# Attention with a LoRA gate, one core: the order of weight splits, low parts and the gate's activation changed

## The reference

```python
xn = _layernorm(x, axis=-1)
# s = attention(xn):
q = rmsnorm(xn @ Wq.T, q_norm_w); k = rmsnorm(xn @ Wk.T, k_norm_w); v = xn @ Wv.T
scores = einsum('bkgqd,bksd->bkgqs', qg, k) / sqrt(HD)
bias = where(rel > 0, NEG_INF, slopes * rel)      # ALiBi, causal
s = (softmax(scores + bias) @ v) @ Wo.T
# g = silu of a mixture of 8 low rank products of xn, weighted by a softmax of a router
g = _silu(_L0_ffn_ref(xn, A, B, Wr, br))
x = x + s * g
```

## Time and profile before

| | before |
|---|---|
| median of 3 runs | 810.39 us (809.46 to 814.38) |
| the profiled execution: its time, its span | 813.82 us, 812.0 us |
| PE busy | 740.5 us (91%) |
| DVE, ACT, POOL busy | 599.1 us (74%), 561.0 us (69%), 403.5 us (50%) |
| DMA, mean share of 16 engines | 63% |
| mean granted clock of TensorE | 0.973 |

### The profile page before, as it was taken

How to read it: one execution, slowest core, us unless ns; L and a number is a source line. 1 busy time by engine, 2 the same in 40 slices (tenths; PEclk the granted TensorE clock), 3 DMA queues, 4 the chain that set the end, 5 groups by cost and what they waited for, 6 DMA issues and landing times.

```text
span 812.0 us, 14699 instructions
## 1 busy us (share of the span) xinstructions
PE 740.5 (91%) x3729; PEld 620.5 (76%) x3729; DVE 599.1 (74%) x1378; ACT 561.0 (69%) x1370; POOL 403.5 (50%) x423
## 2 busy tenths in 40 slices
PE   8888989989899889989899899999899898999787
PEld 7777868867788778878788678877787787887676
DVE  7855677776878778686887769687786768778455
ACT  4665767677677778667676776776685676768763
POOL 5313454456445663554544564544645544446447
PEclk9999999999999999999999899999999999999989
DMA  7014848577485757768486766858476684856732
GB/s 278 1 34 126 272 114 232 165 211 217 128 276 145 230 157 217 205 170 258 116 253 169 197 203 164 263 130 266 133 220 185 179 254 111 264 157 178 237 98 91
DMA packets 214707, 148.27 MB, mean 183 GB/s; under 512 B 48896, under 2 KB 205440, under 8 KB 214528
## 3 DMA queue, kind: packets, MB, share of 16 engines
q1 hardware_dynamic: 214656, 147.77, 63.2%
HBM read 85.84 MB, written 61.87 MB: 182 GB/s over the span
## 4 chain that ended last, share of the span: by engine, by line
PE 31%; issue 20%; DVE 11%; POOL 10%; DMA 10%; ACT 10%; SPq 7%; DVEq 1%; ACTq 0%; POOLq 0%
POOL pt_lo L515 5%; SPq L419 5%; PE qkv_ps L1137 5%; DMA x_sb<-turning 4%; PE qkv_ps L1138 4%; PE qkv_ps L1139 4%; POOL inv_rms L505 3%; ACT probs L633 3%; DMA qk_moved<-turning_qk 3%; PE score_ps L1137 3%; PE score_ps L1139 2%; PE out_ps L1137 2%; PE score_ps L1138 2%; PE out_ps L1138 2%; PE out_ps L1139 2%
## 5 line engine op out<-in xcount | busy, mean ns | idle before, releaser
L515 POOL TENSOR_TENSOR pt_lo<-x_sb,pt_hi 128x512 fp32r<-128x512 f32 x153 | 199.8, 1332 | 229.4 <-ACT pt_hi L677 229.4
L1137 PE MATMUL qkv_ps<-w_hi,xt_hi 128*128 128x512 f32 (+1 forms) x512 | 178.8, 349 | 26.6 <-DVE w_lo L960 19.4
L625 ACT ACTIVATE probs<-probs,neg_max 128x128 f32<-128x128 f32 (+3 forms) x256 | 141.9, 556 | 58.9 <-DVE neg_max L884 56.9
L884 DVE CUSTOM_DVE_ANT_0 probs<-score_ps,cst,slope 128x128 f32<-128x128 f32 (+3 forms) x256 | 131.3, 547 | 63.0 <-PE score_ps L1139 54.2
L1138 PE MATMUL qkv_ps<-w_lo,xt_hi 128*128 128x512 f32 (+1 forms) x512 | 177.2, 346 | 0.0
L1139 PE MATMUL qkv_ps<-w_hi,xt_lo 128*128 128x512 f32 (+1 forms) x512 | 175.9, 343 | 0.0
L1137 PEld LDWEIGHTS qkv_ps<-w_hi,xt_hi 128*128 128x128 f32 x512 | 99.6, 195 | 48.9 <-DVE w_lo L960 22.3
L633 ACT ACTIVATE probs<-probs,recip 128x128 f32<-128x128 f32 (+3 forms) x252 | 122.3, 548 | 9.9 <-DVE recip L891 9.9
L903 DVE STREAM_TRANSPOSE squared<-probs 128x256 f32<-128x256 f32 (+3 forms) x124 | 102.6, 828 | 27.2 <-ACT probs L633 26.7
L1138 PEld LDWEIGHTS qkv_ps<-w_lo,xt_hi 128*128 128x128 f32 x512 | 99.5, 194 | 12.1
L1139 PEld LDWEIGHTS qkv_ps<-w_hi,xt_lo 128*128 128x128 f32 x512 | 99.2, 194 | 11.8
(11 more groups left out here) (157 smaller groups left out, 1424.5 us busy)
## 6 DMA issues: line engine op xcount, KB each, us to landing
turning_qk<-squares SPq DMA_DIRECT2D x240, 80.0 KB, 1.9
qk_moved<-turning_qk SPq DMA_DIRECT2D x60, 320.0 KB, 3.3
turning<-squared SPq DMA_DIRECT2D x120, 128.0 KB, 2.3
x_sb<-turning SPq DMA_DIRECT2D x30, 512.0 KB, 5.1
w_raw<-wqkv SPq DMA_DIRECT2D x32, 384.0 KB, 5.5
turning<-squared SPq DMA_DIRECT2D x120, 96.0 KB, 1.9
x_sb<-turning SPq DMA_DIRECT2D x30, 384.0 KB, 4.3
turning<-squared SPq DMA_DIRECT2D x128, 64.0 KB, 1.7
```

Of the source, the lines that this page charges most:

```text
L515: nc.gpsimd.tensor_tensor(by_quad(pt_lo, j), moved_block(t, j), by_quad(pt_hi, j).bitcast(F32), ALU.subtract).then_inc(pt_lo_by_pool, 1)
L625: nc.scalar.activation(probs[:, h, 0:n], probs[:, h, 0:n], ACT.Exp, bias=neg_max[:, h:h + 1], scale=-1.0, accum_out=total[:, h:h + 1]).the ...
L884: nc.vector.tensor_tensor_reduce(probs[:, h, 0:n], score_bank(t, h), cst[:, C_DIST + SEQ - n:C_DIST + SEQ], slope[:, h:h + 1], HUGE, ALU.a ...
L1137: pe.matmul(out, a_hi, b_hi, start=start, stop=False)
```

## The change

Four things move; nothing is added or removed.

- ACT's `w_hi` of chunks 0 and 1 moves from the end of slot 4 into slot 5, behind squares(7) and `value_hi`, ahead of the exponentials.
- DVE's `w_lo` of chunks 0 and 1 moves, within slot 5, from behind `square_both` to ahead of `value_lo`.
- In every slot q_lo and k_lo of unit t+1 come ahead of the first `square_probs` of unit t.
- In the last group the Silu moves from the end of slot 4 to the end of slot 5, and ahead of slot 6's exponentials ACT now makes o_hi(4); DVE makes `add_out`(3) and o_lo(4) ahead of `reciprocals`(6).

```diff
-SILU_SLOT = 4
+SILU_SLOT = BY_PE - 1
...
# ACT, slot()
                     value_hi(g, t + 2)
+                if w_due:
+                    split_w(g + 1, range(0, EARLY_W))
                 if here(t, left):
                     exponentials(g, t, range(0, HPG))
...
                     moved_hi(g, t - 1)
-                if t % BLOCKS == 4 and here(t + 4, left):
-                    split_w(g + 1, range(0, EARLY_W))
                 if left == 1 and t == SILU_SLOT:
                     gates()
...
# ACT, end()
+                mixed_hi(g, before - 2, 1)
                 exponentials(g, before, range(0, HPG))
...
-                mixed_hi(g, before - 2, 1)
                 turned_qk_hi(g, last)
...
# DVE, slot()
                     bias(g, t, 3)
+                if t % BLOCKS == 5 and here(t + 3, left):
+                    split_w(g + 1, range(0, EARLY_W))
...
                     square_both(g, t + 2)
-                if t % BLOCKS == 5 and here(t + 3, left):
-                    split_w(g + 1, range(0, EARLY_W))
                 if here(t - 3, left):
                     add_out(g, t - 3)
-                if here(t, left):
-                    square_probs(g, t, 0)
                 if here(t + 1, left):
                     turned_qk_lo(g, t + 1)
                 if here(t, left):
+                    square_probs(g, t, 0)
                     square_probs(g, t, 2)
...
# DVE, end()
+                add_out(g, before - 3)
+                mixed_lo(g, before - 2, 1)
                 reciprocals(g, before, 0)
                 reciprocals(g, before, 2)
-                add_out(g, before - 3)
-                mixed_lo(g, before - 2, 1)
```

## The result

| | before | changed |
|---|---|---|
| median of 4 runs each | 811.72 us (809.46 to 814.38) | 825.32 us (820.60 to 829.67) |
| ratio | | 1.0157, 95% interval 1.0105 to 1.0209 |
| the profiled execution: its time, its span | 813.82, 812.0 us | 820.60, 818.8 us |
| PE, DVE, ACT, POOL busy | | 741.7, 583.8, 560.3, 397.0 us |

A second measurement, 11 runs of the same kernel, again beside the kernel before, gave 1.0072 (1.0046 to 1.0098) and a median of 816.67 us. The two intervals don't touch. That the change costs time is in both; how much, 6 or 13 us, I could not settle. The prediction was 806.6 (794 to 816): wrong. A gain was forecast and there is a loss.

The account below looks back on a forecast made before the run. PE, busy 740.5 of 812.0 us, was the bound; idle time and low clock were winnable. -1.6 + 0 - 1.5 + 0.6 + 0.7 = -1.8, and -2 more, gave 810.0 profiled, median 806.6 us, range 794 to 816.

Parts of the forecast that it names:

- The last group: Moved Silu: scores(6) 3.7 us earlier, exponentials(6) later; end moves by -0.3 to +2.5, taken as +0.7 us.
- slot 5: Weights split at project(8): five groups at -1.3 + 0.6, two at +0.35 + 0.6, sum -1.6 us.
- the other slots: First turned copy up to 1 us later elsewhere; 7 groups x 0.2, half met by k_lo's earlier end: +0.6 us.
- slow stretches: Extra gain in some groups because a dropped stretch at 1.2 GHz spares later slots: -2 us.
- the mutual hold-up: Slot 5: DVE's `w_lo` and POOL delay each other, `inv` 0.89 to 1.65 us later; gain 0.9 to 1.7 in five groups.
- what the later read is worth: Slot 5: read of `qk_moved`(7) 0.8 to 1.6 us later, half booked as reaching the path, 0.6 us.
- rival B: Slower: the later `qk_moved`(7) read delays projections in slots 0 and 1; +5 to +10 us, 813 to 820; chance 0.20.
- From slot 2 to 3: k_lo's wait at scores(3) goes, head 3 waits about 4 us, set by o_hi(0) and the branch: gain 0.
- +1 each: Bound at scores(3): the longer single wait may bring a longer slow stretch, +6 us in six groups.
- The -1.5 for the last group's slot 3: No branch in the last group, so copies and o_lo end about 1.5 us earlier there: -1.5 us.

Follow-up runs that it names:

- s_only: Only the last group's Silu moved, with o_hi(4), add_out(3) and o_lo(4) ahead as in the change, against the kernel before: 1.0074.
- wk: Split of chunks 0 and 1 moved and q_lo, k_lo ahead of the first square_probs, Silu as before, against the kernel before: 1.0021.
- w_only: Only the split of chunks 0 and 1 moved, on ACT and DVE, against the kernel before: 1.0008.
- full_again: The whole change measured a second time, 11 runs, against the kernel before: 1.0072, median 816.67 us.
- k_2: q_lo and k_lo ahead of the first square_probs in slot 2 alone, against the kernel before: 0.9964.
- k_701: q_lo and k_lo ahead of the first square_probs in slots 7, 0 and 1 alone, against the kernel before: 1.0000.
- k_46: q_lo and k_lo ahead of the first square_probs in slots 4 and 6 alone, against the kernel before: 1.0037.
- k_5: q_lo and k_lo ahead of the first square_probs in slot 5 alone, against the kernel before: 1.0132.
- k2_ohi: q_lo, k_lo ahead of square_probs in slot 2, and o_hi(0) ahead of wo_hi and the second probabilities there, against the kernel before: 0.9957.
- s_bare: Only the Silu moved to the end of slot 5, o_hi(4), add_out(3), o_lo(4) left behind the exponentials, against the kernel before: 0.9993.
- k_only: q_lo and k_lo ahead of the first square_probs in every slot, nothing else changed, against the kernel before: 1.0139.
- w_ohi: Split of chunks 0 and 1 moved and o_hi(0) ahead of the wo_hi, no new order of q_lo and k_lo, against the kernel before: 0.9950.
- wk2_ohi_first: Split moved, q_lo and k_lo first in slot 2, both probability pairs and o_hi(0) ahead of all wo_hi, against the kernel before: 1.0016.

## Why the prediction was wrong, step by step

The prediction had two blocks of terms, and both were off. The last group was booked at +0.7 us and costs 6.0 (3.2 to 8.8; s_only). All the rest was booked at -4.5 (-1.6 for slot 5, 0 and -1.5 for slot 3, +0.6 for the other slots, -2 for slow stretches) and comes to +1.7 (-1.1 to +4.5; wk). So the two misses are 5.3 and 6.2 us. The mechanism of the first is known. For the second the runs show which steps were wrong, but not the price of each.

**Slot 5, the mutual hold-up: right, and sized right in the group of the rows.** `inv` was to come 0.89 to 1.65 us later and came 1.30 later. Project(8) was to start at T + 3.4 to 4.2 (it started at 583.81, T + 4.0), with a wait of 0.6 to 1.4 (here 0.6), then a wait for chunk 3 (1.13), and end at T + 9.4 to 10.1 (T + 9.7). The read of `qk_moved`(7) was to be 0.8 to 1.6 later and is 1.0 later. What all that is worth, a gain of 0.9 to 1.7 in five groups, no run bears out: w_only, which has this part alone, gained 0.5 a group in slot 5, no more than the same code varies, and lost 0.7 in slot 6. The Trainium skill ("GPSIMD Engine Reference", the row on SBUF interfaces) says that GpSimd shares these with VectorE and that there is contention where VectorE's instruction has two SBUF inputs. The rows agree: `w_lo` has two, and `sums_eps` took 0.91 us beside it in place of 0.22.

**Slot 5, what the later read is worth: wrong.** "I book half of it as reaching the path, 0.6 us, because the same slots have PE work in hand." What counts is the distance to PE, which has itself moved ahead: 3.3 us between the start of scores(6) and the read in place of 0.9 or 2.3, where the rows of the prediction counted from T. Slots 7, 0 and 1 are 1.4 us longer a group (0.7 in full_again and in wk, 0.6 had been booked), and w_only, k_2, k_701 and k_46, in which the read is no later than 2.3 us, have none of it in slot 7. k_5 isolates the place: a larger delay of the same read, without the earlier split, costs 1.3%. How the late read comes to hold head 3's `neg_max` in slots 7 and 0 was not followed step by step. This is rival B's starting point, to which I gave 0.20, but not its chain and not its price. Its sign, waits of over 1 us before the projections of slots 0 and 1, shows in two groups of seven (1.56 and 1.05 in slot 1), and before in one (1.23). Of its 5 to 10 us the end was to make 2.5, and wk, which has all but the end, shows 1.7 (-1.1 to +4.5). That its range of 813 to 820 takes in the 816.67 of the second measurement is mostly luck: 6 us of that loss come from the last group.

**From slot 2 to 3: the step right, the clock on top.** The wait for k_lo goes, head 3's comes, o_hi(0) and the branch set it: k_2, k2_ohi and the "issue" rows show it. The forecast for the slot was 0, with "+1 each" as a bound for a longer slow stretch. Measured were +2.0 in the changed kernel: 0.85 of waiting, which was to be 0, and 1.13 of lower clock. What the forecast missed in the other direction is that slot 5 gives it back: in k_2 PE comes later to slot 5, which is 2.5 us shorter, and the whole is no slower than before (0.9964). One must not sum slots that hand their waits on. The -1.5 for the last group's slot 3, where there is no branch, can't be judged: it is 1.1 us shorter than before (13.64 and 14.71), but in s_only and s_bare, where nothing was changed there, it took 12.79 and 13.92.

**The other slots: right for slots 7, 0 and 1** (k_701 is 1.000). The loss of 11 us by the new order of q_lo and k_lo (k_only) sits in slot 5, where the prediction looked at it together with the earlier split only.

**The last group: the miss whose cause is shown.** "Scores(6) starts near 769.9, 3.7 us earlier": it needed q_hi(6) by that account. On DVE k_lo(6) stands behind all that squares(7) starts (sums, `qk_norm`, its copy, `add_out`), and squares(7) waited for the write of unit 6's q and k, up to the same moment at which SP could read them (768.18 and 768.24). The Silu had hidden that wait. In s_only scores(6) waits 7.34 us, more than before, and in wk, with the Silu in its old place, 5.56: the Silu did not hold scores(6). "ACT is free for it at about 770, so Silu, o_hi(4) and the table load end at 778.4 to 779.1", "+0.7": o_hi(4) needs mix(4), which PE makes behind scores(6) and out(3), with the clock at 0.63 on the mean from 774.8 to 782.4. Counted from the end of project(7), the first exponential of 6 was to come at 18.8 to 19.5 us (it came at 16.2 before) and came at 23.4, and at 24.1 in s_only. ACT was free for the Silu 2.7 us later than booked, because of squares(7), and then waited 3.55 us for mix(4). (The pieces named in the recorded sentence, from 770 on, also add up to 776.8 and not to 778.4; what the rest is it does not say.) And I let what stands behind the exponentials (probabilities, q_hi(7), scores(7)) go almost free. Scores(7) began 16.4 us behind scores(6), where it was 12.3, with a wait of 3.6 us and a slow stretch behind it. This is the step that failed most clearly: 6 us, not 0.7 (s_only), and all of it goes when o_hi(4), with `add_out`(3) and o_lo(4), is put back behind the exponentials (s_bare).

**The 2 us "for what a dropped slow stretch spares later slots"** have no row, and no run shows them: the time at the lower clock is 46 us in the trace of the kernel before and 47 in that of the changed one.

The branch: by the Trainium skill ("Runtime: NRT & Kernel Launch", "Instruction fetch mechanics") a taken branch whose target lies outside the fetched window stalls until the target is fetched. The nearly fixed 3.3 to 3.8 us in k_2, k2_ohi and w_ohi fit that; that it is the fetch, no run here shows.

## What to carry to other kernels

A wait of the busiest engine is only worth the distance to the next thing that it would wait for, and a wait removed in one slot of this pipeline came back in the next or was paid back two slots on (k_2: +2.0 in slot 3, -2.5 in slot 5): measure one group's length, not one gap, and take the spread of the same code from a second trace before reading a difference. Before moving an operation up in an in-order queue, ask what its own input waits for (o_hi(4) on PE's last product) and what stands behind it. And ask of each operation that is pushed back whether a transfer hangs on it; here one turned copy in one of eight slots cost 1.3%.

## What was not expected of the hardware

- A 5-element operation of POOL took 0.91 us beside DVE's `w_lo` in place of 0.22, and `inv_rms` 1.76 in place of 1.17. DVE's q_lo took 1.10 to 2.28 us beside POOL's `w_lo` (1.10 before, 1.74 in k_5, 2.28 in w_only), and 0.65 to 0.69 alone.
- The way over DVE's loop branch takes 3.2 to 3.9 us from the later of two moments, the start of the last turned copy and the end of o_hi(0), to the first operation behind it. That holds for 101 of the 102 passages in 17 traces; the other took 2.95 (wk2_ohi_first).
- After 4 to 4.5 us of standing still at head 3 of scores(3), PE ran at 1.2 GHz (granted clock 0.50) for 3.4 to 6.8 us in each of the six groups of the changed kernel; after its waits of 0.4 to 1.2 us at or inside project(8) it stayed at full clock.
